# Routing by token halves: eight expert blocks of the first half's tokens are written out between the second half's attention and routing

## The chip, the cores and the metric

The kernel runs on one core of one Trainium2 chip. Its time is the device time of one execution, in microseconds (us); of several runs the median is given. Engines: TensorE (PE in the rows; PEld is its weight load), VectorE (DVE), ScalarE (ACT), GpSimd (POOL) and SyncE (SP). Each works through its own list of instructions in order; they wait for each other on semaphores. POOL also issues the indirect DMAs (gather and scatter by a list of row numbers), SP most of the direct ones.

## What is computed

```
x = x + tanh(g_xattn[0]) * graph_attention(ctx, layernorm(x))
x = x + tanh(g_ffn[0])   * ffn(layernorm(x))                      # 256 -> 704 -> 256
x = x + tanh(g_xattn[1]) * sparse_graph(ctx, layernorm(x))        # top 30% of a 256x256 similarity
scores = layernorm(x) @ gate_w.T                                  # 1024 tokens, 8 experts
mult, sel = two best experts of each token and their weights
h = silu(x w1_e.T) * (x w3_e.T);  y_e = h w2_e.T                  # 256 -> 512 -> 256, for expert e
x = x + tanh(g_ffn[1]) * sum over the two experts of mult * y_e
```

x is 4 x 256 x 256 in float32: 1024 tokens of 256 features. Each token goes to two experts, which makes 2048 pairs. For the inputs that are timed, the router gives the experts 0 to 7 these numbers of pairs (counted with the reference): of tokens 0 to 511 137, 163, 139, 104, 90, 144, 102, 145; of tokens 512 to 1023 116, 146, 136, 155, 150, 93, 121, 107; together 253, 309, 275, 259, 240, 237, 223, 252.

## The kernel before

Tokens lie in 8 tiles of 128 rows. Half 0 is tiles 0 to 3, half 1 is tiles 4 to 7; PARTS cuts them into part 0 (tiles 0 to 3), part 1 (4, 5) and part 2 (6, 7). The engines' work up to the router is written out in five lists, PE_ORDER, ACT_ORDER, DVE_ORDER, POOL_ORDER and the code of SP; a step such as ("ffn_down", 1) names a function and its part or half. Half 0 is ahead of half 1: while PE is in the FFN of half 1, DVE does the sparse attention and the second layernorm of half 0 (attn_stats, attn, attn_out, moe_stats, norm_moe), and part 0's router runs at the end of the FFN. Then come ffn_down of parts 1 and 2, the same chain of DVE steps for parts 1 and 2, and their router.

Between these steps DVE also runs a search for the similarity threshold (below), in pieces that FILL places.

Only when all 8 tiles have scores does routing begin, in straight code behind the lists: one-hot matrices of the choices (L1320 to L1334), two small matmuls that count and rank them (L1702, L1703), DVE arithmetic that gives every pair a slot (L1340 to L1380), 16 small bf16 matmuls that turn the slots into a list of token numbers (block_list, L1710), and the list itself, idsu (L1388). A second list of the same form holds the weights (coef).

The expert stage works in blocks of 128 slots. The 16 static blocks are two for each expert (expert j // 2), unrolled. Pairs beyond 256 of one expert go to overflow blocks: one of them always runs, then a loop runs blocks // 2 pairs of further ones, where blocks is the number of overflow blocks that the counts ask for. For one block: POOL gathers 128 rows from xn_rows in DRAM (L547), PE turns them (turn_x, L1724), ACT copies them (L790), PE multiplies with w1 and w3 (up, L1731: 16 matmul passes each), ACT takes silu (L795), DVE multiplies (gate, L1433), PE multiplies with w2 (down, L1740: 8 passes), ACT scales with the weights (L803), and POOL scatters the rows with an addition into the output (L556). Each scatter waits for the one before it to land, since both add to the same tensor. Overflow blocks have other matmul forms (L1746, L1753, L1760) with the expert's place read from a register.

The order within the static stage is:

```
for j in range(FIRST):                       # FIRST = 16
    up(W1[j // 2], 0, q, up1_done)
    if j == 0:
        block_list(1, 3, 3)
    turn_x(1 - q)
    up(W3[j // 2], 2, q, up3_done)
    if j >= 1:
        down(j - 1, 1 - q)
```

SP loads the experts' weights early, except for experts 5 and 6: their place holds the FFN's weights, so these six transfers of 512 KB start when ffn_down is over (down_done). SP also stores x (the output's first value) and xn (the rows to gather) part by part.

Of the kernel before, what the change touches and what calls it, by code (L numbers as in the profile page):

```python
# [6 lines left out]
ALU = mybir.AluOpType  # L7
# [3 lines left out]
P = 128  # L11
B, N, C = 4, 256, 256
T = B * N // P
# [17 lines left out]
FIRST = 2 * E  # L31

OVER = 12
NO = OVER + 3
NL = FIRST + NO
# [20 lines left out]
def build(nc, x_in, ctxT_in, g_xattn, g_ffn, gamma, w0_in, w0T_in, b0_in, w1_in, w1T_in, a_in, b1_in,  # L56
# [5 lines left out]
    with ctx:  # L62
# [3 lines left out]
        def sem(name):  # L66
# [12 lines left out]
        iota_q = sb("iota_q", [P, E])  # L79
        iota_w = sb("iota_w", [P, E])  # L80
# [75 lines left out]
        rs = sb("rs", [P, 3, HT])  # L156
# [28 lines left out]
        O = sb("O", [P, 2, T, E])  # L185
        Os = sb("Os", [P, E, T])
        Dk = sb("Dk", [P, 2, T, E])
        Fk = sb("Fk", [P, 2, T, E])
        second = sb("second", [P, T, E])
        Ek = sb("Ek", [P, 2, T, E])  # L190
        ab = sb("ab", [P, T, E])
        mk = sb("mk", [P, 2 * T])
# [10 lines left out]
        run = sb("run", [P, E, T])  # L203
        same_e = sb("same_e", [P, E, T])
        past = sb("past", [P, E, T])
# [20 lines left out]
        hhT = [hT[:, 2 + q, :] for q in range(2)]
        yv = [hT[:, 4, q * C:(q + 1) * C] for q in range(2)]
# [12 lines left out]
        experts_loaded = sem("experts_loaded")  # L240
# [28 lines left out]
        x3_ready = sem("x3_ready")  # L269

# [38 lines left out]
        rows_stored = sem("rows_stored")  # L309
        out_stored = sem("out_stored")  # L310
# [6 lines left out]
        rank_done = sem("rank_done")  # L317
# [9 lines left out]
        gathered = [sem(f"gathered{q}") for q in range(2)]  # L327
# [1544 lines left out]
```

## Time and profile before

| | us |
|---|---|
| median of 3 runs | 263.69 (262.64 to 264.39) |
| the profiled execution | 262.24 |
| its span in the trace | 260.1 |
| PE busy | 219.7 (84% of the span) |
| DVE, ACT, POOL busy | 120.5, 74.7, 76.1 |
| span of the chain that ended last on PE | 77% |

The profile gives busy time by engine, the granted TensorE clock in stretches (1.00 is 2.4 GHz, 0.50 is 1.2 GHz), groups of instructions by line, and the chain of work that ended last: followed back from the last instruction, at each step to what released it. Starts are us from the start of the span.

### The profile page before, as it was taken

What the parts mean: (1) busy time and instruction counts of PE and PEld (TensorE: products, weight loads), DVE (VectorE), ACT (ScalarE), POOL (GpSimd) and SP (SyncE); (2) the same over time, 40 slices, a digit from 0 to 9 for tenths busy, and PEclk for the clock granted to TensorE, in tenths of its full rate; (3) what the DMA queues carried; (4) which work ended last, traced back from release to release, by engine and by line L of the source; (5) the groups of instructions that cost most, each with busy time, mean ns of one, the idle gap of its engine ahead of it and who ended that gap; (6) DMA issues with size and microseconds to landing.
All of it is one profiled execution on the core that took longest, in us unless ns stands there. A gap on an engine that the chain in (4) does not pass through costs nothing.

```text
span 260.1 us, 3580 instructions
## 1 busy us (share of the span) xinstructions
PE 219.7 (84%) x1240; PEld 174.2 (67%) x1241; DVE 120.5 (46%) x395; ACT 74.7 (29%) x163; POOL 76.1 (29%) x96
## 2 busy tenths in 40 slices
PE   8998989989999989407126999999999999999930
PEld 8687644446854378306115999999999999966620
DVE  0685896599979895884885112111112111111100
ACT  0981468873012210003200222222322222222310
POOL 6006212510001100220013125444554445545440
PEclk9999999999999979955555899999999999999995
DMA  5677169389600310583001004322233222222000
GB/s 163 179 256 221 35 202 355 92 305 415 251 1 0 109 52 4 183 341 121 0 1 60 23 0 61 61 42 44 38 47 53 53 43 37 29 34 27 9 3 1
DMA packets 16258, 25.69 MB, mean 99 GB/s; under 512 B 4141, under 2 KB 11824, under 8 KB 16240
## 3 DMA queue, kind: packets, MB, share of 16 engines
q1 hardware_dynamic: 10304, 19.81, 21.4%
q0 software_dynamic: 4128, 5.25, 11.4%
q10 hardware_dynamic: 1808, 0.40, 0.7%
q8 instruction: 10, 0.16, 0.3%
q14 instruction: 8, 0.07, 0.1%
HBM read 20.86 MB, written 5.64 MB: 102 GB/s over the span
## 4 chain that ended last, share of the span: by engine, by line
PE 77%; DVE 12%; issue 2%; DMA 2%; ACT 2%; POOL 1%; POOLq 0%; ACTq 0%; DVEq 0%
PE PS L1731 23%; PE PS L1630 11%; PE PS L1740 11%; PE PS L1644 9%; PE PS L1746 4%; PE PS L1451 3%; PE PS L1505 3%; PE PS L1683 2%; PE PS L1724 2%; DVE stat L862 2%; PE PS L1503 2%; PE PS L1472 1%; PE PS L1493 1%; PE PS L1760 1%; PE PS L1603 1%
## 5 line engine op out<-in xcount | busy, mean ns | idle before, releaser
L1731 PE MATMUL PS<-hT,e 128*128 128x128 f32 x512 | 64.2, 280 | 0.5 <-ACT hT L790 0.5
L1731 PEld LDWEIGHTS PS<-hT,e 128*128 128x128 f32 x512 | 62.6, 197 | 1.6 <-ACT hT L790 0.9
L1433 DVE TENSOR_TENSOR hT<-th,PS 128x512 f32<-128x512 f32 x19 | 13.1, 688 | 87.5 <-PE PS L1731 72.6
L1630 PE MATMUL PS<-xnT,e 128*128 128x512 f32 x88 | 39.5, 599 | 2.1 <-ACT xnT L751 1.9
L556 POOL DMA_INDIRECT out_dram<-hT,idsu x16 | 25.4, 1589 | 43.4 <-ACT hT L803 37.7
L1630 PEld LDWEIGHTS PS<-xnT,e 128*128 128x128 f32 x88 | 16.1, 190 | 21.3 <-issue 19.6
L1740 PE MATMUL PS<-e,hT 128*128 128x256 f32 x128 | 30.3, 379 | 0.0
L514 POOL TENSOR_TENSOR rstd<-veps,nhalf 128x4 f32<-128x4 f32 (+1 forms) x8 | 7.1, 892 | 65.1 <-DVE veps L871 65.1
L547 POOL DMA_INDIRECT zc<-xn_rows,idsu x16 | 16.9, 1059 | 29.4 <-issue 22.7
L1740 PEld LDWEIGHTS PS<-e,hT 128*128 128x128 f32 x128 | 23.2, 190 | 3.0 <-issue 0.5
L803 ACT ACTIVATE hT<-PS,coef 128x256 f32<-128x256 f32 x19 | 9.0, 474 | 53.5 <-PE PS L1740 45.4
L1644 PE MATMUL PS<-e,hT 128*128 128x256 f32 x96 | 23.0, 402 | 0.0
L1644 PEld LDWEIGHTS PS<-e,hT 128*128 128x128 f32 x96 | 19.2, 202 | 3.3 <-issue 0.5
L795 ACT ACTIVATE th<-PS 128x512 f32<-128x512 f32 x19 | 11.3, 597 | 29.5 <-PE PS L1731 25.9
L772 ACT ACTIVATE th<-PS,gs 128x512 f32<-128x512 f32 (+1 forms) x12 | 8.2, 685 | 29.7 <-PE PS L1630 29.6
L530 POOL DMA_INDIRECT e<-graph_rows,gix x8 | 8.4, 1051 | 22.5 <-DMA graph_rows<-e 15.6
L1724 PE MATMUL PS<-ident,zc 128*128 128x128 f32 x40 | 8.2, 289 | 5.0 <-DMA zc<-xn_rows,idsu 5.0
L790 ACT ACTIVATE hT<-PS 128x256 f32<-128x256 f32 x20 | 7.6, 380 | 14.0 <-PE PS L1724 14.0
L1603 PE MATMUL PS<-ident,xn 128*128 128x128 f32 x16 | 3.3, 357 | 9.6 <-DVE xn L1215 9.6
L1746 PE MATMUL PS<-e,hT 128*128 x24 | 11.3, 593 | 0.0
L1237 DVE SCALAR_TENSOR_TENSOR hT<-th,us,PS 128x512 f32<-128x512 f32 (+1 forms) x12 | 9.0, 747 | 3.0 <-PE PS L1630 2.4
L1451 PE MATMUL PS<-ones 128*128 128x128 f32 x56 | 9.3, 332 | 1.0 <-POOL ones L473 1.0
(242 smaller groups left out, 279.6 us busy)
## 6 DMA issues: line engine op xcount, KB each, us to landing
e<-e_in SPq DMA_DIRECT2D x24, 512.0 KB
x<-x_in SPq DMA_DIRECT2D x2, 512.0 KB, 7.3
graph_rows<-e SPq DMA_DIRECT2D x4, 256.0 KB, 2.5
e<-gw_in SPq DMA_DIRECT2D x1, 768.0 KB
e<-uw_in SPq DMA_DIRECT2D x1, 640.0 KB
e<-dw_in SPq DMA_DIRECT2D x1, 640.0 KB
out_dram<-x SPq DMA_DIRECT2D x1, 512.0 KB, 3.0
xn_rows<-xn SPq DMA_DIRECT2D x1, 512.0 KB, 2.9
```

Of the source, the lines that this page charges most:

```text
L547: pool.indirect_dma_start(out=xg[q], out_offset=None, in_=xn3_dram, in_offset=bass.IndirectOffsetOnAxis(ap=ids, axis=0), bounds_check=boun ...
L556: pool.indirect_dma_start(out=out, out_offset=bass.IndirectOffsetOnAxis(ap=ids, axis=0), in_=yv[q], in_offset=None, bounds_check=bound, oo ...
L795: act.activation(th[:, q, :], PS[:, q, :], ACT.Silu).then_inc(silu_ready, 1)
L803: act.activation(yv[q], PS[:, 6 + q, 0:C], copy, scale=by).then_inc(y_scaled, 1)
L1433: dve.tensor_tensor(hh[me], th[:, me, :], PS[:, 2 + me, :], ALU.mult).then_inc(gated, 1)
L1451: pe.matmul(PS[:, bank, 0:P], ones[:, :], ones[:, :], start=True, stop=True)
L1630: mm = pe.matmul(PS[:, bank, :], w[:, k, it * P:(it + 1) * P], xnT[:, h, k, :], start=(k == 0), stop=(k == 1))
L1644: mm = pe.matmul(PS[:, 4 + i // 2, (i % 2) * 256:(i % 2 + 1) * 256], hT[:, it, i * P:(i + 1) * P], dw[:, it, :], start=(it == 0), stop=(it ...
L1724: mm = pe.transpose(PS[:, 4, q * 256 + k * P:q * 256 + (k + 1) * P], xg[q][:, k * P:(k + 1) * P], ident[:, :])
L1731: mm = pe.matmul(PS[:, bank + q, f * P:(f + 1) * P], w[:, k * F + f * P:k * F + (f + 1) * P], xgT[q][:, k, :], start=(k == 0), stop=(k == 1))
L1740: mm = pe.matmul(PS[:, 6 + q, 0:C], hh[q][:, f * P:(f + 1) * P], W2[j // 2][:, f * C:(f + 1) * C], start=(f == 0), stop=(f == F // P - 1))
L1746: mm = pe.matmul(PS[:, bank + q, :], xgT[q][:, k, :], w[:, bass.ds(at + k * F, F)], start=(k == 0), stop=(k == 1))
```

## The change

Routing is done twice, once for each half. The first list has one column of 128 slots for each expert, filled with pairs of half 0 alone. Pairs of half 0 beyond 128 of an expert (spare) go to the second list, together with the pairs of half 1. The eight blocks of the first list (EARLY: experts 0, 1, 2, 3, 4, 7, 5, 6) are written into the order lists, among the attention, layernorm, router and counting of half 1. Then come seven static blocks (LATE: experts 1 to 7), then expert 0's second block in the overflow form, and then the loop: its pairs of blocks are now (incl + 1) // 2, where incl counts, over the experts, the blocks of 128 that the second list needs beyond the first.

```diff
-FIRST = 2 * E
-OVER = 12
+EARLY = (0, 1, 2, 3, 4, 7, 5, 6)
+LATE = (1, 2, 3, 4, 5, 6, 7, 0)
+STATIC = 2 * E - 1
+OVER = 14
...
-                    ("ffn_up", 1, 5), ("turn_moe", 0), ("router", 0), ("ffn_down", 1), ("lost", 1), ("ffn_down", 2),
-                    ("kept", 1), ("turn_moe", 1), ("turn_moe", 2), ("router", 1), ("router", 2)]
+                    ("ffn_up", 1, 5), ("turn_moe", 0), ("router", 0), ("ffn_down", 1, 0), ("count", 0), ("ffn_down", 1, 1), ("list", 0),
+                    ("lost", 1), ("ffn_down", 2, 0), ("ffn_down", 2, 1),
+                    ("turn_x", 0), ("kept", 1), ("up1", 0), ("turn_x", 1), ("up3", 0),
+                    ("up1", 1), ("turn_x", 2), ("up3", 1), ("down", 0), ("list", 1),
+                    ("up1", 2), ("turn_moe", 1), ("turn_x", 3), ("up3", 2), ("router", 1), ("turn_moe", 2), ("down", 1),
+                    ("up1", 3), ("router", 2), ("turn_x", 4), ("up3", 3), ("count", 1), ("down", 2),
+                    ("up1", 4), ("turn_x", 5), ("up3", 4), ("down", 3),
+                    ("up1", 5), ("turn_x", 6), ("up3", 5), ("list", 2), ("down", 4),
+                    ("up1", 6), ("turn_x", 7), ("up3", 6), ("down", 5)]
...
+                     ("silu", 3), ("copy_x", 4), ("scale_y", 2), ("silu", 4), ("odds", 1), ("copy_x", 5), ("scale_y", 3),
...
+                     ("attn_out", 2), ("gate", 0), ("moe_stats", 2), ("norm_moe", 1), ("shares", 0), ("norm_moe", 2), ("gate", 1),
+                     ("coefs", 0), ("spare", 0), ("choices", 1), ("gate", 2), ("choices", 2),
...
+            def scatter(j):
...
+                pool.wait_ge(y_scaled, j + 1)
+                if j:
+                    pool.wait_ge(scattered, 16 * j)
...
+            def attn_scale(p):
+                t, n = PARTS[p]
+                act.wait_ge(attn_scales, p + 1)
+                for i in range(t, t + n):
+                    ins = act.activation(xr[:, i, :], xr[:, i, :], ACT.Identity, bias=rs[:, 1, i:i + 1], scale=rs[:, 2, i:i + 1])
+                ins.then_inc(x2_scaled, 1)
...
+            def odds(h):
+
+                act.wait_ge(d_ready, h + 1)
+                act.activation(Ek[:, h, :, :, :].rearrange("p k t e -> p (k t e)"),
+                               Dk[:, h, :, :, :].rearrange("p k t e -> p (k t e)"), ACT.Exp, scale=-1.0)\
+                   .then_inc(ek_ready, 1)
+                act.activation(warm[:, :], tg[:, 0:1], ACT.Silu)
...
+            def count(h):
...
+                for s in range(HT):
+                    mm = pe.matmul(to[:, :, 0:HT], before[:, :] if s == 0 else ones[:, :], Os[:, h, :, HT - 1 - s:2 * HT - 1 - s],
+                                   start=(s == 0), stop=(s == HT - 1))
+                for t in range(HT):
+                    mm = pe.matmul(to[:, :, HT], ones[:, :], Os[:, h, :, HT - 1 + t], start=(t == 0), stop=(t == HT - 1))
```

Two pieces of DVE work go to ACT with it: the scaling of x by the attention's layernorm (attn_scale, before four or two DVE instructions a part, L1270) and the second layernorm's output (norm_moe, before L1215). The matmul forms within a block are as before, and the search is placed in other gaps by FILL.

Where the instructions stand. On PE at the end of the FFN, before (L1644 is ffn_down, L1655 lost, L1668 kept, L1603 turn_moe, L1683 router, L1702 the count):

```order
L1683 MATMUL PS<-rg,xnT 128x8 x7
L1644 MATMUL PS<-e2,hT 128x256 [waits down_read,ffn_h_ready]
L1644 MATMUL PS<-e2,hT 128x256 x11
L1655 MATMUL PS<-found,ones 128x1 [waits found_ready,scores_read,xnT_copied]
L1644 MATMUL PS<-e2,hT 128x256 [waits ffn_h_ready]
L1644 MATMUL PS<-e2,hT 128x256 x11
L1668 MATMUL PS<-ident,a2 128x128 [waits a2_ready,scores_read,xnT_copied]
L1668 MATMUL PS<-ident,a2 128x128 x7
L1603 MATMUL PS<-ident,xn 128x128 [waits xn_ready]
```

The same place on PE now (L1796 is ffn_down, L1854 and L1857 the count of half 0, L1874 its list, L1808 lost, L1886 turn_x):

```order
L1796 MATMUL PS<-e2,hT 128x256 x5
L1854 MATMUL PS<-Os,before 128x8x4 [waits ffn_h_ready,onehots_ready]
L1854 MATMUL PS<-Os,ones 128x8x4 x3
L1857 MATMUL PS<-Os,ones 128x8 x4
L1796 MATMUL PS<-e2,hT 128x256 [waits down_read,ffn_h_ready]
L1796 MATMUL PS<-e2,hT 128x256 x5
L1874 MATMUL PS<-RA,h0T 128x16 [waits ph_ready,rh_ready]
L1874 MATMUL PS<-RA,h0T 128x16 x3
L1874 MATMUL PS<-RA,h0T 128x16 [waits ph_ready]
L1874 MATMUL PS<-RA,h0T 128x16 x3
L1808 MATMUL PS<-found,ones 128x1 [waits found_ready,scores_read,xnT_copied]
```

Half 0's count and list stand between the tiles of ffn_down, so the other tiles of ffn_down run while DVE and POOL turn them into gathered rows.

On ACT from the FFN's second step of half 1 on, before (L772 is the FFN's silu, L760 the copy of turn_moe, L783 and L786 the exponentials of routing):

```order
L772 ACTIVATE th<-PS,gs 128x512 [waits ffn_h_ready,ffn_g_done] x5
L772 ACTIVATE th<-PS,gs 64x512 [waits ffn_h_ready,ffn_g_done]
L760 ACTIVATE xnT<-PS 128x1024 [waits ffn_g_done,xnT_done]
L760 ACTIVATE xnT<-PS 128x2x256 [waits ffn_g_done,xnT_done] x2
L783 ACT_TABLE_LOAD
L783 ACTIVATE Ek<-Dk 128x128 [waits d_ready]
L786 ACT_TABLE_LOAD
```

The same place on ACT now (L835 is the FFN's silu, L842 attn_scale, L855 norm_moe, L824 the copy of turn_moe):

```order
L835 ACTIVATE th<-PS,gs 128x512 [waits ffn_h_ready,ffn_g_done] x2
L842 ACTIVATE x<-x,rs 128x256 [waits attn_scales]
L842 ACTIVATE x<-x,rs 128x256 x3
L835 ACTIVATE th<-PS,gs 128x512 [waits ffn_h_ready,ffn_g_done] x2
L855 ACTIVATE xn<-x,ns,rstd 128x256 [waits norm_scales,xnT_done]
L855 ACTIVATE xn<-x,ns,rstd 128x256 x3
L835 ACTIVATE th<-PS,gs 128x512 [waits ffn_h_ready,ffn_g_done]
L835 ACTIVATE th<-PS,gs 64x512 [waits ffn_h_ready,ffn_g_done]
L824 ACTIVATE xnT<-PS 128x1024 [waits ffn_g_done,xnT_done]
L862 ACT_TABLE_LOAD
L862 ACTIVATE Ek<-Dk 128x64 [waits d_ready]
```

Four scalings and four normalisations now stand in front of silus that the FFN waits for.

On POOL, now, around the end of the early blocks (L605 is a gather, L622 a scatter; before, one gather and one scatter alternated throughout):

```order
L622 DMA out_0_dram<-a2,ids_early 1024x256 [waits out_stored0,y_scaled]
L622 DMA out_0_dram<-a2,ids_early 1024x256 [waits y_scaled,scattered] x3
L605 DMA sim<-xn3_rows,ids_late 128x256 [waits rows_stored2,xgT_done,rows_stored1,list_ready,rows_stored0]
L605 DMA sim<-xn3_rows,ids_late 128x256 [waits xgT_done]
L622 DMA out_0_dram<-a2,ids_early 1024x256 [waits y_scaled,scattered]
L605 DMA sim<-xn3_rows,ids_late 128x256 [waits xgT_done]
```

The first gather of the second list stands behind the scatter of early block 3, and the scatters behind it wait for that gather's list.

## Rows read from the trace of the kernel before

**Rows 1.** Windows: stretch and its length, PE, PEld, DVE, ACT, POOL busy, granted clock, DMA.

```profile
77.00:93.60 16.60, 15.29 (x54) 7.75 (x53) 15.40 (x44) 3.77 (x5) 2.02 (x2) 1.00 0.18 63
94.00:98.00 4.00, 4.00 (x13) 3.17 (x12) 3.66 (x16) 0.00 (x0) 0.00 (x0) 0.57 0.00 0
106.10:116.50 10.40, 0.89 (x9) 0.66 (x6) 9.78 (x31) 0.00 (x0) 2.18 (x4) 0.74 0.88 327
106.10:139.50 33.40, 9.63 (x55) 7.78 (x52) 26.74 (x104) 4.63 (x7) 4.53 (x6) 0.57 0.37 134
152.30:229.40 77.10, 77.10 (x589) 74.21 (x589) 9.63 (x14) 18.85 (x42) 37.35 (x30) 1.00 0.28 44
229.40:250.10 20.70, 19.74 (x76) 12.43 (x74) 2.06 (x3) 5.98 (x13) 10.57 (x12) 1.00 0.15 16
```

**Rows 2.** Chain that ended last, in order of time: start, us, what; the gap.

```profile
106.16 0.70 DVE x L1246
...
133.08 0.40 PE PS L1710 x4
...
135.45 2.85 DMA zc<-xn_rows,idsu
...
139.58 3.78 PE PS L1731 x16
```

**Rows 3.** The same chain, two static blocks and two overflow blocks.

```profile
171.06 1.79 PE PS L1731 x16
...
176.57 1.79 PE PS L1731 x16
...
235.13 1.72 PE PS L1746 x4
...
240.95 1.72 PE PS L1746 x4
```

**Rows 4.** Timeline: start, us, engine, line; small PE work, and the FFN's wait.

```profile
87.70 1.98 PE L1630 MATMUL PS<-xnT,e 128*128 128x512 f32 x4 [0.20 <-DVE hT L1237]
...
91.80 1.95 PE L1683 MATMUL PS<-rg,xnT 128*128 128x8 f32 x16 [1.11 <-ACT xnT L760]
...
105.96 1.04 PE L1668 MATMUL PS<-ident,a 128*128 128x128 f32 x8
...
131.37 0.36 PE L1710 MATMUL PS<-RH,sim 128*128 128x62 bf16 x4 [6.30 <-DVE sim L1380]
```

**Rows 5.** Groups of ACT instructions by form, 40 to 60 us: count, busy us, mean ns.

```profile
L685 ACT ACTIVATE a<-sim,bar 128x256 f32<-128x256 f32 x16 | 7.9, 497 | 0.0
```

**Rows 6.** Timeline: the exponential between two table loads on ACT.

```profile
124.41 0.31 ACT L783 ACTIVATE Ek<-Dk 128x128 f32<-128x128 f32 x1 [3.67 <-DVE Dk L1334]
...
124.74 1.28 ACT L786 ACT_TABLE_LOAD   x1
...
126.03 0.20 ACT L786 ACTIVATE warm<-tg 128x1 f32<-128x1 f32 x1
```

**Rows 7.** Timeline of DVE: one scaling; first and last of the weights' arithmetic (13 rows).

```profile
109.82 0.74 DVE L1270 TENSOR_SCALAR x<-x,rs 128x256 f32<-128x256 f32 x2
...
135.12 0.22 DVE L1397 SCALAR_TENSOR_TENSOR ab<-sc 128x64 f32<-128x64 f32 x1
...
138.49 1.84 DVE L1419 TENSOR_TENSOR RH<-RH,parts 128x496 bf16<-128x496 bf16 x3
```

**Rows 8.** Timeline of POOL: scatters (L556, L579) and what waited for their landing.

```profile
192.53 1.58 POOL L556 DMA_INDIRECT out_dram<-hT,idsu  x1 [2.58 <-ACT hT L803]
...
198.19 1.59 POOL L556 DMA_INDIRECT out_dram<-hT,idsu  x1 [2.73 <-DMA out_dram<-hT,idsu]
...
236.54 1.59 POOL L556 DMA_INDIRECT out_dram<-hT,idsu  x1 [1.72 <-ACT hT L803]
...
240.58 0.19 POOL L575 COPY sidx<-idsu 128x1 uint32 x1 [0.38 <-DMA out_dram<-hT,idsu]
...
252.66 1.58 POOL L579 DMA_INDIRECT out_dram<-hT,sidx  x1 [0.91 <-POOL sidx L575]
```

More of the change, by code:

```diff
@@ L1632, in ffn_up, with ffn_down @@
                     mm.then_inc(ready, 1)
-            def ffn_down(p):
+            def ffn_down(p, only=None):
                 t, n = PARTS[p]
@@ L1685, in router @@
                 mm.then_inc(scores_done, 1)
-            steps = dict(mix=mix_weights, queries=queries, sims=sims, weights=weights, hidden=hidden, feat=graph_feat,
-                         hot=graph_hot, choice=choice, compose=compose, stay_warm=stay_warm,
-                         flag=graph_flag, graph_check=graph_check, turn_ffn=turn_ffn, ffn_up=ffn_up, ffn_down=ffn_down, lost=lost, kept=kept,
-                         turn_moe=turn_moe, router=router)
-            pe.wait_ge(ones_ready, 1)
@@ L1788, in _ @@
-            half_way = FIRST // 2
-            pe.wait_ge(eoff_ready, 1)
-            at = expert(0)
-            pe.wait_ge(xgT_copied, FIRST + 1)
-            pe.wait_ge(gated, FIRST - 1)
-            up_over(e1, 0, 0, at, up1_done)
-            pe.wait_ge(gathered[1], 16 * (half_way + 1))
-            turn_x(1)
-            up_over(e3, 2, 0, at, up3_done)
-            down(FIRST - 1, 1)
+            steps = dict(count=count, list=block_list, turn_x=turn_x, up1=up1, up3=up3, down=down, mix=mix_weights, queries=queries, sims=sims, weights=weights, hidden=hidden, feat=graph_feat,
+                         hot=graph_hot, choice=choice, compose=compose, stay_warm=stay_warm,
+                         flag=graph_flag, graph_check=graph_check, turn_ffn=turn_ffn, ffn_up=ffn_up, ffn_down=ffn_down, lost=lost, kept=kept,
+                         turn_moe=turn_moe, router=router)
@@ new lines, in _ @@
+            pe.wait_ge(ones_ready, 1)
+            open_clock_gate(WARM_UP, 7)
+            pe.wait_ge(consts, CONSTS)
+            for name, *at in PE_ORDER:
+                if name in steps:
+                    steps[name](*at)
+            for j in range(7, STATIC):
+                up1(j)
+                if j == 7:
+                    block_list(3)
+                turn_x(j + 1)
+                up3(j)
+                down(j - 1)
+            pe.wait_ge(eoff_ready, 1)
+            pe.wait_ge(coef_ready, 2)
```

851 lines of the change are left out of this document (478 added, 373 removed).

## The prediction

> **What bounds the kernel now.** I read the windows by stage first, then the chain of waits in order of time, then the timelines of PE, DVE and POOL in the stretch between FFN and experts. Up to 106.1 us PE is nearly always busy: from 77.0 to 93.6, in the FFN's second half, 15.29 of 16.60 us [rows 1]. From 152.3 to 250.1 it is busy for 96.8 of 97.8 us, at full clock. Between them, 106.1 to 139.5, lie 33.4 us in which PE has 9.63 us of work, at a mean granted clock of 0.57, while DVE is busy for 26.7 [rows 1]. The chain in that stretch goes through DVE's attention and layernorm of parts 1 and 2, the router, the count, DVE's slots, the list that ends at 133.48 and the first gather that lands at 138.3, to the first block at 139.58 [rows 2]. So routing is a wait on a chain, not a load on an engine, and only work of PE that doesn't depend on it can fill it. Eight blocks of half 0 are such work.
>
> **The block.** A static block takes 176.57 - 171.06 = 5.51 us of PE, an overflow block 240.95 - 235.13 = 5.82 [rows 3]. Before, 16 static and 3 overflow blocks run: experts 1, 2 and 3 are above 256 pairs, so 3 overflow blocks are asked for, one always runs, and 3 // 2 = 1 pair follows.
>
> **Blocks afterwards.** The second list holds max(first half - 128, 0) + second half: 125, 181, 147, 155, 150, 109, 121, 124 for experts 0 to 7. Four are above 128, so incl = 4 and (4 + 1) // 2 = 2 pairs run behind 15 static blocks and expert 0's block: 20 blocks where there were 19. The change itself costs a block, since splitting the tokens pads more. 15 x 5.51 + 5 x 5.82 = 111.8 us.
>
> **Until the first block.** Before, ffn_down ends at 106.1.
> - Four scalings and four normalisations of 128x256 move from DVE to ACT, in front of silus. The nearest ACT row is 0.50 us each [rows 5], so 2.0 us for each group of four, ahead of a silu. The FFN had little slack there: its last step already waits for DVE's product, for 0.20 us at 87.70 [rows 4]. The first group holds up the product of the FFN step behind it by about 3 us, of which PE's lead of two steps covers 2; the second delays turn_moe by 2.2, and the copy now stands behind two silus. I take 2.5 us until the end of part 0's router (bounds 0, if the lead covers it, and 4, the two groups in full).
> - count of half 0: 8 matmuls, 16 passes, as the router's 16 in 1.95 us [rows 4]: 2.0. list of half 0: 8 passes, by the 0.36 for 4 at half clock [rows 4], 0.5.
> - Clock: from 94 to 98 it is 0.57 already, behind the wait and the small matmuls of the router [rows 1, 4]. Now there are more waits and a second group of small matmuls. I take 1.2 us more (bounds 0 and 4, the present stretch once more at half clock).
> - DVE's arithmetic, the index list and the gather: before, 138.3 - 133.5 = 4.8 us lie between list and gathered rows [rows 2]. Now the two last tiles of ffn_down (5.3 us) stand there, so this is hidden with about 1 us to spare at the DVE steps in between; if that cover is gone, PE waits for the excess.
>
> First turn_x at 106.1 + 2.5 + 2.0 + 0.5 + 1.2 = 112.3.
>
> **Work put between the blocks.** kept 1.0 [rows 4], list 0.4, turn_moe 0.9, routers 2.0, count 2.0, the two long lists 1.0 each (16 passes each at the 0.06 to 0.09 of [rows 4]): 8.3 us. They were in the gap before, at half clock; now they are on PE's path.
>
> **Stalls between the blocks.** DVE needs, from the end of ffn_down, what it did in 10.4 us from 106.1 to 116.5 [rows 1], without the 2.2 us of scaling and normalising (two tiles in 0.74 [rows 7], three times), plus a gate (0.7) and the weights of half 0: 5.2 us for both halves [rows 7], about 3.4 for one with its narrower lists. That is 12.3 us, until list 1 may start; PE has turn_x, kept, four ups and a down, some 10.6. Stall 1.7. Then the exponential of half 1 stands on ACT between silu 4 and copy_x 5, with a table load on each side: 1.28 + 0.31 + 1.28 + 0.20 = 3.1 us [rows 6], then 0.38 for the copy; PE has up3 and down, 3.5, less the silu's 0.6 and hand-overs: stall 0.5. The last block's turn through ACT costs 1.0, as before (20.70 less 19.74 in the last stretch [rows 1]). Together 3.2. Here the rows show a switch of tables as 1.31 us, with the next instruction right behind [rows 6]. The Trainium skill (ScalarE: Activation LUTs, What ACT_TABLE_LOAD costs) puts a drain of 1.38 us to each load; by it the pair of switches would be 2.8 us longer, the sum would be 2.8 higher, and it speaks against placing them there. The trace has no such drain.
>
> **Tail.** From PE's last matmul at 250.1 to the end are 10.0 us: scale, the wait for the scatter before, and the last scatter, from 252.66 to 260.1 [rows 8]. The last blocks are small overflow blocks again; I keep 10.0.
>
> **Sum.** 112.3 + 111.8 + 8.3 + 3.2 = 235.6 for PE's end, where it was 250.1; with the tail 245.6 of span. The profiled execution took 262.24 with a span of 260.1, so 2.1 more: 247.7. The median is 263.69, 1.45 above that execution. So 249.2, a ratio of 0.945. The gap gave up 33.4 us; 5.8 go to the block, 8.3 to work now on the path, 6.2 to the later start, 2 to stalls.
>
> **What else could happen.**
> - *The scatters become the bound.* Each waits for the one before it to land, and each next one starts 0.9 us after. One landed by 240.5, 3.9 after its start, but that of 192.53 held the next until 198.19: 5.66 start to start, over a block's 5.51 [rows 8]. Now POOL's list also keeps scatter 4 behind the first gather of the second list, which waits for list 2 on PE (about 151.6): scatter 4 at about 155.7, and 15 follow. At 5.7 and 5.8 each the last starts at 242.3 instead of 238.2, plus 7.4 to the end: 253.3. For it: two of 14 scatters were held this way. Against: the other twelve landed in time, and the first early scatters have slack. 15%.
> - *DVE or ACT is late in the early blocks.* They interleave attention, two routers, count and slots with gates; any step waits in order. The margins above are 1 to 2 us in a row of some ten hand-overs. If half of them are missed, 2 to 8 us: about 254. This is also the case in which the first gather is late and the early blocks don't start where they should. 12%.
> - *A table switch costs more when ACT has work queued than when it is idle, as it was in [rows 6]*: if each of the two loads costs twice its 1.28, PE waits 2.6 longer at block 5: 251.8. The trace speaks against it. It is the rule of the page on ScalarE named above, by another price. 4%.
> - *The clock stays at its lower level.* It did from about 111.5 to 145 [rows 1, 2], with 3.78 us for the 16 passes that take 1.79 later [rows 3], once PE had been idle. The Trainium skill (TensorE: Matmul & The Clock Gate, What's actually happening) has the low level as the default, which activity lifts. If stalls keep PE there among the early blocks, each us of work costs one more: 4 us gives 253 (5%). **Slower than before** it is when over 14 us of the early blocks' work runs at the half level: 249.2 + 14.5 = 263.7, with all 44 us it would be 293. Against: between 112 and 165 PE should be idle for under 4 us in all, where it was idle for 24 of 33. 5%.
> - *Better*: the hops on ACT are covered and the clock holds: 3.7 less, 245.5. 9%.
> - *The forecast*: 246.5 to 252, 50%.
>
> **The numbers.** 249 is the likeliest. From 244.5 (both free, with a little margin) to 256.5 (scatters and half of the late hand-overs) I leave out the worst of the late cases and the clock: 8 in 10. About 1% can be told from no change here. All cases but the clock in full and a pile of late hand-overs are faster by more: 0.91; within 1% 0.04; slower 0.05.
>
> **What would show it.** Right: PE busy for over 85% of every stretch from 106 to 230; first up of an expert at about 113; 20 silus of the expert stage; last matmul near 236; a clock of 1.00 from 115 on. Where a step is wrong: turn_x waiting for a gather or list 1 for DVE beyond 2 us; up1 of block 5 waiting for ACT by 3 us (the drain); router of part 0 later or earlier than 96; scatter starts 5.7 apart with "<-DMA" as releaser, and turn_x of block 18 waiting for its gather (the scatters). The prediction would be wrong as a whole if 18 or 22 blocks ran, or if the early blocks ran at 0.50.

## The result, and the profile after

| | before | after |
|---|---|---|
| median beside each other, us | 263.16 (261.11 to 264.39, 4 runs) | 251.77 (247.88 to 255.44, 4 runs) |
| ratio, 95% interval | 1 | 0.950 (0.942 to 0.958) |
| the profiled execution, and its span | 262.24, 260.1 | 252.58, 250.6 |
| PE busy | 219.7 (84%) | 227.6 (91%) |

Two more sets of runs of the same changed kernel, taken later with the experiments, gave medians of 249.25 (6 runs, ratio 0.950, 0.946 to 0.954) and 250.74 (6 runs, 0.952, 0.944 to 0.960). The middle of all 16 executions is 250.1; they spread over 7.7 us, those of before over 4.5 (one of 596.46 us left aside). The ratios compare the faster executions of each kernel alone, those within 1.5% of its fastest, which is why 0.950 isn't 251.77 / 263.16 = 0.957. The kernel is 5% faster. The forecast was 249.2.

The windows of after, against those of [rows 1] (stretch and length, then PE, PEld, DVE, ACT, POOL busy, clock, DMA):

```profile
77.00:93.60 16.60, 13.89 (x39) 5.91 (x37) 13.34 (x39) 7.04 (x13) 2.02 (x2) 1.00 0.14 49
93.60:106.10 12.50, 11.92 (x56) 10.88 (x57) 7.40 (x38) 1.81 (x2) 0.00 (x0) 0.73 0.06 20
106.10:230.00 123.90, 119.52 (x827) 105.69 (x826) 45.34 (x166) 36.57 (x76) 53.13 (x49) 0.97 0.30 68
120.00:140.00 20.00, 16.07 (x104) 14.61 (x104) 7.63 (x43) 5.81 (x13) 8.52 (x8) 0.83 0.43 126
```

The gap of before, 24 us idle in 33.4 [rows 1], is gone: from 106.1 to 230 PE is idle for 4.4 us in all. Of these 3.9 lie between 120 and 140, where the clock is 0.83 and PE is busy for 80%.

PE's timeline of after, at the places that the sum went by (start, us, engine, line; in brackets the idle time before it and what ended it):

```profile
76.18 1.06 PE L1821 MATMUL PS<-ident,a 128*128 128x128 f32 x8 [0.36 <-DVE a L1102]
...
85.15 3.70 PE L1781 MATMUL PS<-xnT,e 128*128 128x512 f32 x8 [1.04 <-DVE hT L1331]
...
91.86 1.09 PE L1831 MATMUL PS<-ident,xn 128*128 128x128 f32 x8 [0.78 <-ACT xn L855]
94.18 3.58 PE L1841 MATMUL PS<-rg,xnT 128*128 128x8 f32 x16 [1.24 <-ACT xnT L824]
97.62 4.46 PE L1796 MATMUL PS<-e,hT 128*128 128x256 f32 x12
...
103.62 2.84 PE L1796 MATMUL PS<-e,hT 128*128 128x256 f32 x12
106.29 0.35 PE L1874 MATMUL PS<-RA,h0T 128*128 128x16 bf16 x8
...
111.98 0.38 PE L1886 MATMUL PS<-ident,sim 128*128 128x128 f32 x2
...
124.71 0.36 PE L1874 MATMUL PS<-RA,h0T 128*128 128x24 bf16 x8 [1.89 <-issue]
...
238.59 1.99 PE L1942 MATMUL PS<-e,hT 128*128 x8 [0.94 <-ACT hT L888]
```

Router 0 starts at 94.18, where it was 91.80 [rows 4]; its 16 passes take 3.58 us and the 12 passes of ffn_down behind it 4.46, the same 12 passes 2.84 later: half clock. The first turn_x is at 111.98 and waits for nothing, list 1 waits 1.89, PE ends at 240.58.

The chain of waits of after, from 120 to 140 (start, us, what):

```profile
126.30 4.47 another core or an unknown queue
...
130.79 0.61 ACT xnT L824
...
131.44 1.72 PE PS L1841 x8
133.16 0.95 PE PS L1831 x4
134.11 3.41 PE PS L1922 x8
137.53 2.29 PE PS L1900 x16
```

This was in no part of the forecast. ACT is done with scale_y 0 at 126.30 and stands still until 130.79, before the copy behind turn_moe of part 1 (ACT copies what PE has turned, and router 1 reads the copy), although that turn stands at 126.80 to 127.40 in PE's timeline. PE has up3 of block 2 meanwhile, then waits 2.04 us for the copy, and until about 138 works at half clock: 3.41 us for a down of 1.73.

### The profile page after: what moved, and what is told of

Its sections match the earlier page's. It is cut to its first block, busy times and chain, and to the rows that moved or that the text cites. A ratio compares the mean times of both kernels' runs of the same rounds, so it can differ in the third digit from the quotient of the medians.

```text
span 250.6 us, 3835 instructions
## 1 busy us (share of the span) xinstructions
PE 227.6 (91%) x1286; PEld 177.8 (71%) x1287; DVE 122.5 (49%) x428; ACT 87.7 (35%) x188; POOL 79.6 (32%) x103
## 4 chain that ended last, share of the span: by engine, by line
PE 73%; DVE 7%; issue 6%; ACT 6%; another core or an unknown queue 2%; POOL 2%; DMA 1%; DVEq 0%; POOLq 0%; ACTq 0%
PE PS L1900 17%; PE PS L1781 10%; PE PS L1922 10%; PE PS L1796 7%; PE PS L1928 7%; PE PS L1611 4%; PE PS L1942 3%; PE PS L1665 3%; PE PS L1841 2%; DVE stat L956 2%; PE PS L1663 2%; PE PS L1632 1%; PE PS L1653 1%; PE PS L1886 1%
## 5 line engine op out<-in xcount | busy, mean ns | idle before, releaser
L1900 PE MATMUL PS<-hT,e 128*128 128x128 f32 x480 | 59.0, 277 | 0.4 <-ACT hT L869 0.4
L1900 PEld LDWEIGHTS PS<-hT,e 128*128 128x128 f32 x480 | 57.4, 194 | 1.5 <-ACT hT L869 0.8
L1922 PEld LDWEIGHTS PS<-e,hT 128*128 128x128 f32 x120 | 22.9, 200 | 3.2 <-issue 0.5
L1796 PE MATMUL PS<-e,hT 128*128 128x256 f32 x96 | 23.2, 402 | 0.0
L1796 PEld LDWEIGHTS PS<-e,hT 128*128 128x128 f32 x96 | 19.2, 203 | 3.2 <-issue 0.5
L622 POOL DMA_INDIRECT out_dram<-a,ids_early x8 | 12.7, 1593 | 24.0 <-ACT a L898 23.1
L1928 PE MATMUL PS<-e,hT 128*128 (+1 forms) x40 | 18.8, 592 | 0.0
L622 POOL DMA_INDIRECT out_dram<-a,ids_late x7 | 11.0, 1575 | 22.9 <-ACT a L898 22.6
L605 POOL DMA_INDIRECT sim<-xn_rows,ids_early x8 | 8.5, 1059 | 20.9 <-DVE ids_early L1554 19.0
L835 ACT ACTIVATE th<-PS,gs 128x512 f32<-128x512 f32 (+1 forms) x12 | 8.1, 679 | 16.8 <-PE PS L1781 16.7
L1331 DVE SCALAR_TENSOR_TENSOR hT<-th,us,PS 128x512 f32<-128x512 f32 (+1 forms) x12 | 9.0, 747 | 5.0 <-PE PS L1781 2.4
L644 POOL DMA_INDIRECT out_dram<-a,sidx x5 | 7.9, 1586 | 10.0 <-ACT a L903 7.9
L1928 PEld LDWEIGHTS PS<-e,hT 128*128 128x128 f32 x40 | 7.2, 190 | 5.0 <-issue 4.8
L898 ACT ACTIVATE a<-PS,coef_early 128x256 f32<-128x256 f32 x8 | 3.8, 472 | 19.2 <-PE PS L1922 19.2
L1942 PE MATMUL PS<-e,hT 128*128 x40 | 9.5, 381 | 0.9 <-ACT hT L888 0.9
```

The lines of the kernel that those rows point to most:

```text
L605: pool.indirect_dma_start(out=xg[j % E], out_offset=None, in_=xn3_dram[0:(HN, B * N)[h], :], in_offset=bass.IndirectOffsetOnAxis(ap=ids[h] ...
L622: pool.indirect_dma_start(out=out, out_offset=bass.IndirectOffsetOnAxis(ap=ids[h][:, at:at + 1], axis=0), in_=yv[kept_in(j)], in_offset=No ...
L1331: dve.scalar_tensor_tensor(out=hT[at:P, it, :], in0=th[at:P, n % 2, :], scalar=us[at:P, it:it + 1], in1=PS[at:P, bank, :], op0=ALU.mult, o ...
L1796: mm = pe.matmul(PS[:, 4 + a // 2, (a % 2) * 256:(a % 2 + 1) * 256], hT[:, it, a * P:(a + 1) * P], dw[:, it, :], start=(it == 0), stop=(it ...
L1900: mm = pe.matmul(PS[:, bank + q, f * P:(f + 1) * P], w[:, k * F + f * P:k * F + (f + 1) * P], xgT[q][:, k, :], start=(k == 0), stop=(k == 1))
L1922: mm = pe.matmul(PS[:, Y_BANK, q * C:(q + 1) * C], hh[q][:, f * P:(f + 1) * P], W2[expert_of(j)][:, f * C:(f + 1) * C], start=(f == 0), st ...
```

## Experiments

| run | median us (runs) | first turn_x | PE's end | between |
|---|---|---|---|---|
| changed, the three profiles | 251.8, 249.3, 250.7 | 112.0, 113.1, 114.7 | 240.6, 238.4, 240.1 | 128.6, 125.3, 125.4 |
| silu 2 before the copy | 251.0 (4) | 111.3 | 236.6 | 125.2 |
| part 0 scaled on DVE | 250.2 (4) | 113.2 | 238.5 | 125.3 |
| 24 matmuls before router 0 | 254.0 (4) | 112.8 | 241.5 | 128.6 |
| gathers 4 to 7 held | 249.6 (4) | 114.5 | 237.4 | 122.9 |
| scatter 0 behind gather 4 | 250.5 (1) | 113.8 | 238.5 | 124.6 |
| blocks behind routing | 275.9 (5) | 145.2 | 261.5 | 116.3 |
| 18 blocks | 239.1 (4) | 111.2 | 224.9 | 113.6 |
| list 1 later | 251.4 (6) | 113.0 | 239.5 | 126.6 |
| list 1 later, gathers held | 246.6 (6) | 112.8 | 234.5 | 121.7 |
| that, and PE kept busy | 244.6 (6) | 111.2 | 232.9 | 121.7 |

Times from the start of the span; the end is that of PE's last matmul. The forecast had 112.3, 235.6, and 123.3 between them.

**Is the overlap the gain?** All of PE's, ACT's and VectorE's steps of the early blocks moved behind the second half's attention, routing and list 2; the two lists stay. PE then also waits until list 1's weights are read (coef_ready) ahead of turn_moe 2 and of list 2.

```diff
-PE_ORDER: ... ("up1", 0), ... ("list", 1), ("up1", 2), ("turn_moe", 1), ... ("router", 1), ...
+PE_ORDER: ... ("list", 1), ("turn_moe", 1), ("router", 1), ... ("count", 1), ("list", 2),
+          ("turn_x", 0), ("up1", 0), ... ("up3", 6), ("down", 5)
```

> Two lists as in the changed kernel, but PE's, ACT's and VectorE's steps of the eight early blocks stand behind all of the second half's attention, routing and list 2, so nothing overlaps. Main theory (the gain is the overlap alone): list 2 is over about 27.4 us after ffn_down (106.1 to 133.5 in the kernel before), so at about 139.5; from there 20 blocks, 111.8, list 3 and the last block, 2.0: PE ends at 253, the span is 266 and the time 267 to 269, 2% over the kernel before, at a clock of 0.5 to 0.6 from 114 to 143. Rival (smaller lists and the move to ACT gain by themselves): first block below 134, time under 262.

275.93 us, ratio 1.053 (1.048 to 1.059). Windows and PE's timeline of this run:

```profile
112.00:145.00 33.00, 10.86 (x68) 9.66 (x66) 21.96 (x99) 8.58 (x14) 8.21 (x9) 0.54 0.43 148
```

```profile
109.79 1.67 PE L1745 MATMUL PS<-e,hT 128*128 128x256 f32 x7
...
144.57 0.80 PE L1826 MATMUL PS<-RB,h0T 128*128 128x48 bf16 x16 [8.35 <-DVE RB L1422]
145.20 0.67 PE L1838 MATMUL PS<-ident,sim 128*128 128x128 f32 x2
```

The old gap is back, 33 us with 10.9 of work at a clock of 0.54. My 139.5 for list 2 was 6 us too early. The end of ffn_down (L1745) isn't the reason: 139.5 had it at 112.1, and it is at 111.46. The chain behind it is longer: from there to the end of the last list 33.9 us, where I had taken over the 27.4 of the kernel before. Part of this lies ahead of the count, since the two routers now run one after the other (the last one ends 19.4 us behind ffn_down, before 15.9); the rest lies between it and the list. The rest of the miss of 8 us lies behind it: 116.3 us from the first turn_x to PE's end, where I had 113.8, with the first block still at half clock. So smaller lists and the move to ACT gain nothing by themselves; without the overlap the kernel is 5% slower than before, and the overlap is worth 275.9 - 250.1 = 25.8 us (27 by the two ratios, each taken beside the kernel before).

**What a block costs.** The loop runs one pair less.

```diff
-own(dve.tensor_scalar(blocks[:, 0:1], incl[:, E - 1:E], 1.0, None, ALU.add))
+own(dve.tensor_scalar(blocks[:, 0:1], incl[:, E - 1:E], -1.0, None, ALU.add))
```

> The loop's number of pairs is one less (1 instead of 2), so 18 blocks run instead of 20; the rows of the two last overflow blocks are left out of the output. The prediction's step: an overflow block costs 5.82 us of PE and the tail stays, so 11.6 us less than the changed kernel: 238 to 240. Rival (the scatters set the end: each waits for the one before): then one scatter cycle for each, 2 x 5.7 or less than 10 us where they catch up, 240.5 to 243.

239.05 us, 11.1 below the middle of the changed kernel (9 by the ratios, 0.915 against 0.950; the times spread too much to tell these apart). The profiles are sharper: the stretch from the first turn_x to PE's end, where its profile has the same waits as the changed kernel's at 125.3, is 113.6: 5.85 us a block. The term held, and the scatters added nothing.

**What holds the copy back?** First the kernel again, and the silu of block 2 put before the copy on ACT.

> The changed kernel, unaltered, once more. In its profile ACT stood still for 4.49 us before the copy behind turn_moe of part 1 (126.30 to 130.79), though PE's turn had ended by 127.4; PE then waited 2.04 us for that copy and worked at half clock for about 7 us. Theory A (the standstill is an event of single executions, its place or its occurrence varies): a second profile shows it elsewhere or not at all; without it the profiled time is about 247, and the times of single executions lie in 247 to 248 without it and 251 to 255 with it. Theory B (it belongs to this program: order, queue or semaphore): it is at the same instruction again, 4 to 5 us long, and the median stays at 251 to 252.

> On ACT silu of early block 2 stands before the copy of turn_moe 1 instead of behind it; nothing else is changed. Theory B1 (the standstill belongs to the copy: what releases it is late): silu 2 runs at once at about 127, gate 2 follows, the copy still starts at about 130.8, PE's router 1 still waits about 2 us, time within 1 us of the changed kernel. Theory B2 (ACT's own stream stands still at this point of its list, whatever stands there): silu 2 now starts at about 130.8 and the copy behind it at 131.3, PE waits 2.5 us or more, time 0 to 1 us longer. Theory A (an event of single executions): no standstill at this place, time 3 to 5 us below the profiled 252.6, so 247 to 249.

```diff
-ACT_ORDER: ... ("turn_moe", 1), ("silu", 2), ("turn_moe", 2)
+ACT_ORDER: ... ("silu", 2), ("turn_moe", 1), ("turn_moe", 2)
```

249.25 and 251.02 us. The standstill is no chance: it is in both profiles, 4.51 us in the kernel run again, and in the second the silu runs at 127.41 while the copy still waits until 130.09. So ACT itself doesn't stand still: what releases the copy is late (theory B1). The wait of 2 us at router 1 that B1 named didn't come, though: it was 0.34, behind an up1 of block 2 that took 3.02 us, partly at half clock; and the median is 1.8 above that of the kernel beside it, not within 1. In five profiles the copy starts 1.99 to 2.07 us after scatter 0 starts on GpSimd, the last of six issues that stand there in a row. Next, GpSimd's row was changed:

```diff
             def gather(j):
+                if j == HT:                      # gather 4
+                    pool.wait_ge(scores_read, 2)
```

> Gathers 4 to 7 and with them scatter 0 are held on GpSimd until VectorE has read router 1's scores (about 133); nothing else changes, and these gathers land at about 139, when turn_x 4 needs the first of them. In four profiles of kernels with this place the copy behind turn_moe 1 starts 2.06 us after the start of scatter 0 (128.73 and 130.79; 129.85 and 131.92; 129.61 and 131.67), although PE's turn stands 2 to 3.4 us earlier in the timeline, and every semaphore step of PE's turn_moe 1, turn_x 3 and up3 of block 2 is late by it. Theory P (what GpSimd issues there, five gathers and a scatter in a row, keeps these steps back): the copy starts within 0.5 us of the end of turn_moe 1, at about 127.5 to 130, router 1 is not waited for or by under 0.5 us, and the kernel is 1 to 4 us faster than the changed one (2.0 us of waiting and up to 3.4 of half clock), 246 to 248.5. Theory Q (nothing to do with GpSimd, it is PE or ACT at this point): the copy starts about 4.5 us after the end of scale_y 0 as before, and the time stays at 249 to 252.

```diff
-POOL_ORDER: ... ("gather", 4), ("gather", 5), ("gather", 6), ("gather", 7), ("scatter", 0)
+POOL_ORDER: ... ("gather", 4), ("scatter", 0), ("gather", 5), ("gather", 6), ("gather", 7)
```

> On GpSimd scatter 0 stands behind gather 4 instead of behind gather 7, so it starts at about 126.4 (when scale_y 0 is done) and not at 128.7. Theory P1 (the copy behind turn_moe 1 waits for something that ends with scatter 0): the copy starts 2.06 us after the scatter again, at about 128.5, and router 1 is not late. Theory P2 (it waits until all of the row of issues on GpSimd is over, or for the transfers of gather 7): still 130.8 or a little later. Theory Q (not GpSimd): 4.5 us after the end of scale_y 0, 130.8.

With gathers 4 to 7 held (timelines of ACT, PE and VectorE):

```profile
129.90 0.60 ACT L826 ACTIVATE xnT<-PS 128x512 f32<-128x512 f32 x1 [1.13 <-PE PS L1833]
```

```profile
129.26 0.60 PE L1833 MATMUL PS<-ident,xn 128*128 128x128 f32 x4
...
131.70 0.96 PE L1843 MATMUL PS<-rg,xnT 128*128 128x8 f32 x8
```

```profile
141.03 0.69 DVE L1579 TENSOR_TENSOR hT<-th,PS 128x512 f32<-128x512 f32 x1 [1.85 <-PE PS L1902]
```

The copy follows the turn at once, router 1 isn't waited for, and 122.9 us lie between the first turn_x and PE's end. The row stands at 133.72 to 140.56 now, and there it does the same where PE doesn't wait: gate 3 on VectorE starts at 141.03, 2.10 us after the start of the scatter that ends the row, though up3 of block 3 stands in PE's timeline until 139.51. With scatter 0 moved forward the row is broken in two and the copy follows its turn too (130.93, the turn ends at 130.89); that turn was itself late behind passes at half clock, so this run doesn't tell P1 from P2, and it is a single execution. The median of the run with the gathers held, 249.64, shows no gain: its first turn_x came at 114.5, behind two stretches of half clock ahead of it, and in the kernel run again the wait at router 1 was only 0.41, since the slow stretch had begun before it (up1 of block 2 took 2.92 us). The wait and the slow clock hide each other, so this run alone proves the place, not its price. Moving list 1 out of its wait was to tell the price:

```diff
-("up3", 1), ("down", 0), ("list", 1), ("up1", 2), ("turn_moe", 1), ("turn_x", 3)
+("up3", 1), ("down", 0), ("up1", 2), ("turn_moe", 1), ("list", 1), ("turn_x", 3)
```

> On PE list 1, which waited 1.9 us for VectorE's shares, stands behind turn_moe 1 instead of ahead of up1 of block 2, so up1 of block 2 runs in its place; GpSimd's row of five gathers and a scatter is as in the changed kernel. Theory P (PE's semaphore steps are held back until 2.0 us after the start of the last issue of that row): the copy behind turn_moe 1 still starts 2.0 us after the start of scatter 0, at about 131, the 1.9 us saved come back as waiting at router 1 (3 to 4 us there where the clock is high), and the time is within 0.7 us of the changed kernel's, 249 to 251. Theory Q (the steps are late for another reason, with PE's own place): they move forward with PE's work and 1.5 to 2 us are gained, 247.5 to 249.

> The same move of list 1, and gathers 4 to 7 held on GpSimd until router 1's scores are read, so that no row of issues stands beside turn_moe 1. Theory P: neither list 1 nor router 1 is waited for by over 0.5 us; from the first turn_x to PE's last matmul 121 us (123.3 in the forecast's sum, 122.9 in the run with the gathers held alone, less 1.9), and the time is 1.5 to 3.5 us below the changed kernel's, 246 to 248. Theory Q: as with list 1 moved alone, within 0.7 us of that run.

> The changed kernel unaltered, as a measure for the three runs beside it on the same chip: 249 to 252 by its runs so far (249.25 and 251.77 median).

Beside 250.74 for the changed kernel on the same chip (ratio to before 0.952, 0.944 to 0.960), list 1 moved alone gives 251.40 (0.959, 0.953 to 0.965), no faster, and moved with the gathers held 246.63 (0.940, 0.932 to 0.947). Timelines of the first of the two, of PE, GpSimd and VectorE:

```profile
126.55 0.35 PE L1874 MATMUL PS<-RA,h0T 128*128 128x24 bf16 x8
...
132.01 1.18 PE L1841 MATMUL PS<-rg,xnT 128*128 128x8 f32 x8 [2.92 <-ACT xnT L824]
```

```profile
128.41 0.99 POOL L605 DMA_INDIRECT sim<-xn_rows,ids_early  x1 [0.30 <-issue]
132.35 1.63 POOL L622 DMA_INDIRECT out_dram<-a,ids_early  x1 [2.96 <-issue]
```

```profile
130.41 0.17 DVE L1561 COPY coef_early<-PS 128x8 f32<-128x8 f32 x1 [4.10 <-remote]
```

Here VectorE waits for PE's list 1, which stands at 126.55 to 126.90, until 130.41, again with no releaser that the trace shows. The last issue of the row is now gather 7, at 128.41, since the scatter waits for VectorE: 130.41 is 2.00 us behind it. So here it is the row that matters, not the scatter, and whatever PE has finished since about 127 is known to the other engines only then. The 1.9 us came back as a wait of 2.92 at router 1. With the row gone they are a gain: 4.8 us between the two runs, 2.9 of waiting and about 1.7 of half clock behind it.

The row alone isn't enough, though. In the run with the blocks behind routing the same five gathers stand in a row too (120.89 to 126.18), beside a PE that has little work (timelines of PE, GpSimd and VectorE):

```profile
125.47 1.87 PE L1792 MATMUL PS<-rg,xnT 128*128 128x8 f32 x8 [0.69 <-issue]
126.18 1.00 POOL L554 DMA_INDIRECT sim<-xn_rows,ids_early  x1 [0.30 <-issue]
127.45 0.17 DVE L1338 COPY sc<-PS 128x16 f32<-128x16 f32 x1 [1.91 <-PE PS L1792]
```

Router 1 ends at 127.34 and VectorE has its scores 0.11 us later, 1.27 us after the start of the last gather; nothing is late. What the wait takes besides the row is not shown.

**ACT's scalings.** Part 0's scaling and normalisation back on VectorE:

```diff
-ACT_ORDER: ("attn_scale", 0), ("ffn_up", 1, 2), ("ffn_up", 1, 3), ("norm_moe", 0), ("ffn_up", 1, 4)
+ACT_ORDER: ("ffn_up", 1, 2), ("ffn_up", 1, 3), ("ffn_up", 1, 4)
```

> The scaling and the normalisation of part 0 are back on DVE, as in the kernel before; those of parts 1 and 2 stay on ACT. The prediction's step: these eight ACT instructions delay the end of part 0's router by 2.5 us (bounds 0 and 4). If it is right the router of half 0 starts 1.5 to 2.5 us earlier (92 instead of 94.2) and the kernel is 2 to 3 us faster, about 249. Rival (DVE is as late as ACT, since it has the search pieces and the products to do as well): the router starts within 0.5 us of 94.2 and the time is within 1 us of the changed kernel's. A second rival: the clock, low behind the router's waits, is kept up if the wait at 93 goes: then 3 us more are gained, 246.

250.18 us, within 1 us of the changed kernel's 249.25 beside it. PE's timeline of this run, and one row of the kernel before. Their first rows are kept 0, the last work on PE that stands ahead of the scalings in all three kernels; the changed kernel has it at 76.18:

```profile
78.06 1.06 PE L1829 MATMUL PS<-ident,a 128*128 128x128 f32 x8 [0.36 <-DVE a L1102]
...
87.29 3.70 PE L1789 MATMUL PS<-xnT,e 128*128 128x512 f32 x8 [1.30 <-DVE hT L1331]
...
93.11 1.09 PE L1839 MATMUL PS<-ident,xn 128*128 128x128 f32 x8
95.32 2.30 PE L1849 MATMUL PS<-rg,xnT 128*128 128x8 f32 x16 [1.11 <-ACT xnT L824]
```

```profile
76.14 1.06 PE L1668 MATMUL PS<-ident,a 128*128 128x128 f32 x8 [0.35 <-DVE a L1008]
```

From kept 0 to router 0 lie 15.66 us before, 18.00 in the changed kernel and 17.26 here: of the 2.34 us that the order cost, 0.74 came back, where 1.5 to 2.5 were forecast. (By the clock of the span the router starts no earlier, since this execution was already 1.9 us behind at kept 0.) The wait of 0.78 ahead of turn_moe 0 is gone; the one for VectorE's product is still there, 1.30 us instead of 1.04. The run undid the engine, not the place: in VectorE's list too the scaling, and a piece of the search, now stand ahead of the FFN's product (L1331), where before the product came first. That the rest of the cost follows this place is argued; putting it back was not run.

**The clock.** 24 matmuls before router 0 (24 matmuls in float32 are 48 passes):

```diff
-("turn_moe", 0), ("router", 0), ("ffn_down", 1, 0)
+("turn_moe", 0), ("fill", 24, 4), ("router", 0), ("ffn_down", 1, 0)
```

> 24 matmuls of 128x128 on constants stand between turn_moe 0 and router 0, where PE waits 1.24 us for the copy; they fill PE for about 24 x 0.056 = 1.3 us if they pass at the rate of small matmuls at full clock (the clock dropped at about 94.0, behind the waits of 0.78 and 1.24 us, and router 0 took 3.58 us for 16 passes that took 1.95 before). Theory C (the wait at 92.9 to 94.2 brought the clock down): clock stays 1.00 until 106, router 0 takes 1.8 us, ffn_down 2.85 instead of 4.46, first up 3 us earlier, time 3 us below the changed kernel. Rival D (the three waits since 84 together, 2.1 us, or the router's small matmuls themselves bring it down): clock still 0.5 for about 7 us from 94 or somewhat later, time the same or up to 1 us longer.

```profile
93.03 5.52 PE L1611 MATMUL PS<-ones 128*128 128x128 f32 x48
98.39 1.85 PE L1848 MATMUL PS<-rg,xnT 128*128 128x8 f32 x16
100.10 2.84 PE L1803 MATMUL PS<-e,hT 128*128 128x256 f32 x12
...
132.32 1.81 PE L1848 MATMUL PS<-rg,xnT 128*128 128x8 f32 x8 [2.04 <-ACT xnT L824]
```

The clock held (1.85 and 2.84 us), but I had priced a matmul at one pass of 0.056 us instead of two of 0.115: the filling took 5.5 us of a wait of 1.24, so it cost 4.3 and gave back 3.3. The first turn_x stands at 112.8, among those of the changed kernel; what makes 254.0 is behind it, the full wait of 2.04 at router 1 with half clock after it, 128.6 between, as in the first profile. Twelve matmuls, sized to three waits and added to the better of the runs above:

```diff
-("ffn_up", 1, 4), ("ffn_up", 1, 5), ("turn_moe", 0), ("router", 0)
+("fill", 4), ("ffn_up", 1, 4), ("ffn_up", 1, 5), ("fill", 3), ("turn_moe", 0), ("fill", 5), ("router", 0)
```

> As the run with the gathers held and list 1 moved, and small matmuls on constants in three waits of PE at the end of the FFN: 4 (8 passes) ahead of its step 4 (wait 1.04 us), 3 ahead of turn_moe 0 (0.78) and 5 ahead of router 0 (1.24), at 0.115 us a pass as measured, so 0.92, 0.69 and 1.15 us: they cost nothing. Theory C (those waits bring the clock down at 94 to 98 us, for 3.4 to 6.8 us of time at half rate): the stretch at half clock is gone or shorter, and 1.7 to 3.4 us are gained over that run, 244 to 246. Rival D (it takes more, or comes back later at the counts or the lists): no difference, 246 to 248.

244.59 us (243.25 to 245.40), ratio 0.932 (0.926 to 0.938): better than both kernels. Window and PE's timeline:

```profile
93.60:106.10 12.50, 12.27 (x91) 11.18 (x90) 8.99 (x40) 4.19 (x6) 0.00 (x0) 1.00 0.13 43
```

```profile
93.34 0.83 PE L1613 MATMUL PS<-ones 128*128 128x128 f32 x6
...
95.22 1.28 PE L1613 MATMUL PS<-ones 128*128 128x128 f32 x10
96.61 1.95 PE L1847 MATMUL PS<-rg,xnT 128*128 128x8 f32 x16
98.42 2.84 PE L1802 MATMUL PS<-e,hT 128*128 128x256 f32 x12
```

No stretch at half clock is left there. From the FFN's step 4 to the first turn_x lie 23.6 us (87.58 to 111.16), without the filling 26.9 (85.85 to 112.77); behind it both take 121.7. The median is 2.0 us below the run without the filling, and its times lie within 2.2 us of each other; the two intervals overlap (up to 0.938, from 0.932), so that the place is shown by the timelines and its price is about 2 to 3 us.

## Why the prediction was right, point by point

- **Blocks.** 20 silus of experts run. From up1 to up1 a static block takes 5.52 us and an overflow block 5.82, in the chain of after:

```profile
158.34 1.78 PE PS L1900 x16
...
163.86 1.78 PE PS L1900 x16
...
225.57 1.72 PE PS L1928 x4
...
231.39 1.72 PE PS L1928 x4
```

- **Until the first turn_x**: 112.3 forecast, 111.98, 113.08 and 114.70 in three profiles. The later two are late by as much at kept 0 already; the third has a stretch at 0.50 from 25.3 to 28.3 us, in code that the change doesn't touch. The order of the scalings cost 2.4 until router 0's start (forecast 2.5 to its end, 94.18 against 91.80). The clock cost more: router 0 and the tile of ffn_down behind it took 3.58 + 4.46 where 1.95 + 2.84 is full speed, 3.3 us; before had lost 1.7 (4.0 us at 0.57 [rows 1]), so 1.5 more where I had 1.2. The count took 1.7 (2.0), the list 0.35 (0.5). The gather was hidden, as said.
- **Work between the blocks**: 8.3 forecast. The two long lists took 0.40 and 0.52 in the chain instead of 1.0 each; I had taken the price from passes at half clock. This is 1.1 too much; the second count took 0.3 less and the two routers 0.4 less than priced. By PE's rows of the run with the gathers held the work between the blocks adds up to about 6.5.
- **Stalls**: list 1 waited 1.89 (1.7 forecast), the last block cost 0.94 (1.0). Up1 of block 5 waited 0.37 (0.5), behind this row of ACT:

```profile
148.68 1.28 ACT L862 ACT_TABLE_LOAD   x1
149.97 0.26 ACT L862 ACTIVATE Ek<-Dk 128x64 f32<-128x64 f32 x1
150.25 1.28 ACT L865 ACT_TABLE_LOAD   x1
```

  Each load takes 1.28 us between busy neighbours, as when ACT was idle [rows 6]. The rival of a dearer switch fell. The drain of 1.38 us that the Trainium skill (ScalarE: Activation LUTs, What ACT_TABLE_LOAD costs) adds to a load is not there: 0.01 to 0.02 us lie between the rows.
- **Missing: the wait at router 1.** I priced every wait by what the engines have to do, the order lists had six issues in a row on GpSimd, and I didn't ask what they do to the other engines. It cost the profiled execution 2.04 us and, with the half clock behind it, about 3.6 more (0.9, 0.5, 1.7 and 0.5 in the last four PE rows of the chain above, against full speed). These 5.6 are the difference between 128.6 and the 122.9 us of the run with the gathers held (5.7); the forecast was 123.3. In the two other profiles of the kernel the same place cost 2.4 (125.3 and 125.4), 0.4 to 0.5 of waiting and 1.7 of half clock, which begins before router 1 there. The missing term is what put the profiled execution above the forecast: 252.58 where the sum had 247.7.
- **Luck in the sum.** The other terms came to 122.9 against 123.3, but not each of them: the work between the blocks was priced 1.8 too high, and the blocks with the ends of their matmuls came to about 1.3 more than 111.8. The waits fit (3.25 in that run, 3.2 forecast). The medians of 249.25, 250.74 and 251.77 lie so near 249.2 because these errors, the missing wait and the spread of the start partly cancel. The breakdown behind the sum doesn't add up either: 33.4 less 5.8, 8.3, 6.2 and 2 is 11.1, while PE's end was to move by 250.1 - 235.6 = 14.5. Left out is what the first block of before lost at half clock, which lasts until 145 (3.78 us instead of 1.79 for one up alone [rows 2, 3]).
- **The clock** was to be 1.00 from 115 on. It was 0.83 from 120 to 140, and the sign of PE busy for over 85% of every stretch failed there too (80%). The rival of a low clock, 4 us among the early blocks (5%), is what happened in the profiled execution in substance; the other two profiles lost less of it, but started later. Both make the times of executions differ; how much of the spread is theirs, three profiles can't tell. The Trainium skill (TensorE: Matmul & The Clock Gate, What's actually happening) calls the low level the default that activity lifts; the runs with and without filling agree.
- **The scatters** were no bound. Timeline of GpSimd, after:

```profile
183.20 1.63 POOL L622 DMA_INDIRECT out_dram<-a,ids_late  x1 [0.30 <-issue]
187.86 1.60 POOL L622 DMA_INDIRECT out_dram<-a,ids_late  x1 [3.03 <-ACT a L898]
...
242.79 1.57 POOL L644 DMA_INDIRECT out_dram<-a,sidx  x1 [2.16 <-DMA out_dram<-a,sidx]
```

  One follows another after 4.66 us here, where the profile names ACT's scale, 0.9 before, as what it waited for, and after 4.59 and 4.54 in the runs with the gathers held and with the filling, against a block's 5.52; so the row catches up instead of falling behind. The 5.66 of [rows 8] and the other pair that was held before (209.08 and 214.93, 5.85) are the long ones. Only the last waits for a landing.
- **Tail**: 240.6 to 250.6 is 10.0 us, and 2.0 from the span to the time, as forecast.
- **Chances.** 0.91 on faster was not too much: the overlap alone was worth 25.8 us, far more than the terms in doubt.

## What to carry to other kernels

A wait on a chain of arithmetic that no engine is full in can be filled with independent work written between its steps, even where that work grows by a block: price the gap that is left, not the work that is added. Read the order on every engine, GpSimd's too: beside a busy PE, a row of DMA issues without a pause went with news of PE's work that reached the others late, and breaking the row up cured it. Where PE must wait a microsecond ahead of small matmuls, matmuls on constants of just that length can pay for themselves, and passes, not instructions, have to be counted.

## What the runs showed of the hardware

- While GpSimd issued five or six indirect DMAs at 1.3 us each without a pause, what PE had finished became known to ACT and VectorE only 2.0 us after the start of the last one (1.99 to 2.21 in ten profiles with scatter 0 as the last, 2.00 with gather 7). The longest delay was 3.5 us, for list 1 in the run with only that moved. It concerned the last part of the row alone: a silu on PE's product still ran on time 5.9 us after the first issue (127.41, the row from 121.51). Beside the rows of two and four issues of the run with scatter 0 moved no such wait is seen, nor beside the row of five in the run with the blocks behind routing, where PE had little to do (0.11 us from router 1's end to VectorE's read). Why, and whether it is the number of issues, of their descriptors or what PE does meanwhile, stays open; no run varied one of them alone. The profile names it "remote" or "another core or an unknown queue". That such a step is not seen in an engine's own row fits the Trainium skill (Perfetto Trace Analysis, The 4-stage abstract model), which has the update of a semaphore as a stage of its own behind the execution.
- An addition scattered into DRAM (128 rows of 1 KB) that waits for the one before it can start again after 4.54 to 4.66 us, and after 3.95 between the last two; two pairs of the kernel before took 5.66 and 5.85.
- Two waits of 0.78 and 1.24 us, with 16 passes of a small matmul behind, stood ahead of a fall of PE to half clock in three of three profiles of the changed kernel, and one wait of 1.11 before [rows 4]. Filling the wait of 1.24 alone, with 24 matmuls that took 5.5 us, kept the clock up, and so did 12 matmuls in these two and in one wait ahead.
